# A fused attention and expert kernel: weight halves of batch 1 kept in DRAM for batches 2 and 3, and another order of reads and routing steps on VectorE

## What is computed

```python
def _L1_xattn_ref(x, context, Wq, Wkv, null_kv, Wout, ln_scale, ln_bias):
    q = _split_heads(jnp.einsum('bnd,df->bnf', x, Wq))
    kv = jnp.einsum('bmc,cf->bmf', context, Wkv)
    k, v = jnp.split(kv, 2, axis=-1)
    ...
    k = jnp.concatenate((nk, k), axis=-2)
    v = jnp.concatenate((nv, v), axis=-2)
    sim = jnp.einsum('bhid,bhjd->bhij', q * scale, k)
    attn = jax.nn.softmax(sim, axis=-1)
    out = jnp.einsum('bhij,bhjd->bhid', attn, v)
    out = jnp.einsum('bnf,fd->bnd', out.transpose(0, 2, 1, 3).reshape(b, -1, INNER), Wout)
    ...
x = x + jnp.tanh(g_xattn[1]) * _L1_xattn_ref(_layernorm(x, axis=-1), ctx_2048, ...)
x = x + jnp.tanh(g_ffn[1]) * _L1_ffn_ref(_layernorm(x, axis=-1), ...)
```

## Time and profile before

| | us |
|---|---|
| median of 3 runs | 1813.59 (1813.05 to 1813.76) |
| the profiled execution, its own time | 1819.89 |
| its span, first to last instruction | 1818.2 |

### The profile page before, as it was taken

How to read it: one execution, slowest core, us unless ns; L and a number is a source line. 1 busy time by engine, 2 the same in 40 slices (tenths; PEclk the granted TensorE clock), 3 DMA queues, 4 the chain that set the end, 5 groups by cost and what they waited for, 6 DMA issues and landing times. The chain is left out here.

```text
span 1818.2 us, 28277 instructions
## 1 busy us (share of the span) xinstructions
PE 1675.6 (92%) x9558; PEld 1135.1 (62%) x9558; DVE 1244.6 (68%) x2892; ACT 1076.3 (59%) x2214; POOL 421.2 (23%) x422
## 2 busy tenths in 40 slices
PE   5899998899799899999998999999998889999998
PEld 3445554455455344446665666566665788999997
DVE  3867876877778667576768667776685688666632
ACT  2467666666666655666656556566565466667621
POOL 2101110120011011020102010401021467777721
PEclk8899999999999999999999999989999999999999
DMA  3000000000002009320102010201012647777775
GB/s 104 1 24 1 1 24 1 1 24 7 1 1 104 36 1 311 112 67 18 42 18 65 19 39 30 89 18 41 13 43 87 215 135 225 207 216 193 220 228 163
DMA packets 143567, 142.88 MB, mean 79 GB/s; under 512 B 10816, under 2 KB 135744, under 8 KB 143424
## 3 DMA queue, kind: packets, MB, share of 16 engines
q1 hardware_dynamic: 135696, 132.41, 23.2%
q0 software_dynamic: 7152, 8.66, 2.7%
q10 hardware_dynamic: 576, 0.00, 0.0%
HBM read 112.18 MB, written 29.77 MB: 78 GB/s over the span
## 5 line engine op out<-in xcount | busy, mean ns | idle before, releaser
L1273 DVE TENSOR_REDUCE l_tile_max<-psum 128x1 f32<-128x512 f32 x512 | 342.0, 688 | 110.5 <-PE psum L951 108.8
L1121 ACT ACTIVATE l_probs<-psum 128x1024 f32<-128x1024 f32 x256 | 248.3, 1022 | 106.1 <-PE psum L963 102.3
L951 PE MATMUL psum<-l_kT,l_qT 128*128 128x512 f32 x512 | 238.1, 472 | 40.2 <-DVE l_tile_max L1273 36.8
L2047 ACT ACTIVATE l_probsT<-psum 128x1024 f32<-128x1024 f32 x128 | 131.1, 1024 | 140.2 <-PE psum L1926 135.1
L2973 POOL TENSOR_TENSOR moe_w_lo<-moe_w,moe_w_hi 128x512 fp32r<-128x512 f32 x128 | 179.4, 1403 | 95.2 <-ACT moe_w_hi L2757 94.1
L951 PEld LDWEIGHTS psum<-l_kT,l_qT 128*128 128x128 f32 x512 | 98.1, 193 | 132.1 <-DVE l_tile_max L1273 111.6
L2191 DVE TENSOR_REDUCE l_row_max<-psum 128x2 f32<-128x1024 f32 x124 | 151.0, 1218 | 35.5 <-PE psum L1763 35.0
L1983 ACT ACTIVATE l_probs<-psum,l_neg_max 128x512 f32<-128x512 f32 x248 | 168.3, 679 | 0.0
L963 PE MATMUL psum<-l_qT,l_kT 128*128 128x512 f32 x512 | 160.5, 397 | 1.7 <-ACT l_probs L1121 1.5
L2788 ACT ACTIVATE moe_gate<-psum 128x256 f32<-128x256 f32 (+1 forms) x184 | 64.6, 351 | 158.6 <-PE psum L2686 97.7
L2686 PE MATMUL psum<-moe_xs_hi,moe_w_hi 128*128 128x256 f32 x512 | 148.1, 289 | 1.6 <-DVE moe_xs_lo L2814 1.6
(11 more groups left out here) (394 smaller groups left out, 3496.8 us busy)
## 6 DMA issues: line engine op xcount, KB each, us to landing
moe_w<-in_moe_w SPq DMA_DIRECT2D x276, 256.0 KB, 4.7
moe_sorted_x<-l_null_cols SPq DMA_DIRECT2D x1, 17680.0 KB, 56.2
moe_w<-in_wkv SPq DMA_DIRECT2D x6, 1024.0 KB, 5.2
moe_w<-in_wkv SPq DMA_DIRECT2D x24, 256.0 KB, 2.7
moe_xs<-moe_sorted_x SPq DMA_DIRECT2D x16, 272.0 KB
moe_w<-in_ctx SPq DMA_DIRECT2D x8, 512.0 KB, 3.6
moe_w<-in_wkv SPq DMA_DIRECT2D x2, 2048.0 KB, 15.6
moe_w<-in_wq SPq DMA_DIRECT2D x24, 128.0 KB, 2.3
```

Of the source, the lines that this page charges most:

```text
L951: nc.tensor.matmul(bank(max_bank(m)), qT[:, q % SLOTS, h, t * P:(t + 1) * P], kT[:, q % SLOTS, h // 2, half * BANK:(half + 1) * BANK], sta ...
L1121: nc.scalar.activation(probs[:, n % PT_RING], wide(2 * (n % 2)), ACT.Exp, scale=SCALE).then_inc(exp_done, 1)
L1273: nc.vector.reduce_max(tile_max[:, q % 2, t, h, half:half + 1], bank(max_bank(m)), AX_X).then_inc(max_read, 1)
L2047: nc.scalar.activation(probsT[:, m % 2], wide(4).rearrange("p (j n) -> p j n", j=2), ACT.Copy).then_inc(pT_ready, 1)
```

## The change

- In batch 1, after a group's halves are made, SyncE writes them to three new DRAM tensors (`keep_queries`, `keep_keys`, `keep_values`), and waits for these writes before the buffers are loaded anew.
- In batches 2 and 3 SyncE loads hi and lo directly (two DMAs in place of one, twice the bytes), and TensorE waits for the loads. ScalarE's rounding and VectorE's subtractions for queries and keys end with group 15, GpSimd's for the values with batch 1.
- In batch 1 the subtraction for the values moves from GpSimd to VectorE: four instructions of 128x512 at (5, 2), (5, 3), (6, 1), (6, 2) of batch 0 and four at (2, 0) to (2, 3) of batch 1. GpSimd keeps the copies.
- VectorE reads the fill (i, 2, 1) before `extra` rather than behind it.
- In batches 1 and 2 `token_statistics` for the router moves from (5, 2), (5, 3), (6, 0) to (6, 1), (6, 2), (6, 3), and `route_tokens` from (6, 1), (6, 2) to (7, 0), (7, 1).

```diff
                 def load_queries(i):
+                    slot, p = i % 2, i % PAIRS
+                    if i >= 2 * PAIRS:
+                        sp.dma_start(wq_hi[:, slot].bitcast(F32), kept_wq[p, 0]).then_inc(wq_in[slot], 16)
+                        sp.dma_start(wq_lo[:, slot].bitcast(F32), kept_wq[p, 1]).then_inc(wq_in[slot], 16)
+                    else:
+                        cols = slice(p * P, (p + 1) * P)
+                        sp.dma_start(wq_raw[:, slot], dram["wq"][:, cols].rearrange("(c p) n -> p c n", p=P)).then_inc(wq_in[slot], 16)
...
+                def keep_queries(i):
+                    sp.wait_ge(wq_split, i - PAIRS + 1)
+                    sp.dma_start(kept_wq[i % PAIRS, 0], wq_hi[:, i % 2].bitcast(F32)).then_inc(wq_kept, 16)
+                    sp.dma_start(kept_wq[i % PAIRS, 1], wq_lo[:, i % 2].bitcast(F32)).then_inc(wq_kept, 16)
...
                 for n in range(PAIRS - 1, GROUPS):
                     b, p = divmod(n - 2, PAIRS)
+                    new = PAIRS <= n < 2 * PAIRS
                     coming = (n + 1, n + 2) if n == PAIRS - 1 else (n + 2,) if n + 2 < GROUPS else ()
+                    if new:
+                        keep_queries(n)
                     sp.wait_ge(misc_psum, last_fill("q", n))
+                    if new:
+                        sp.wait_ge(wq_kept, 32 * (n - PAIRS + 1))
                     for i in coming:
                         load_queries(i)
+                    if new:
+                        keep_keys(n)
...
                 def project_queries(i):
                     p = i % PAIRS
-                    if i >= PAIRS:
+                    if i >= 2 * PAIRS:
+                        pe.wait_ge(wq_in[i % 2], 16 * (PAIRS // 2) + 32 * ((i - 2 * PAIRS) // 2 + 1))
+                    elif i >= PAIRS:
                         pe.wait_ge(wq_split, i - PAIRS + 1)
...
                 def round_soon(i):
                     b, p = divmod(i, PAIRS)
-                    if PAIRS <= i + 2 < GROUPS:
+                    if PAIRS <= i + 2 < 2 * PAIRS:
                         round_keys(i + 2)
...
-                def split_values(b, half):
+                def round_values(b, half):
                     pool.wait_ge(wv_in, 16 * (2 * (b - 1) + half + 1))
                     for c in range(s.CC):
-                        nc.gpsimd.tensor_copy(wv_hi[:, c, :], wv_raw[:, c, :])
-                    pool.drain()
-                    for c in range(s.CC):
-                        nc.gpsimd.tensor_tensor(wv_lo[:, c, :], wv_raw[:, c, :], wv_hi[:, c, :].bitcast(F32),
-                                                ALU.subtract).then_inc(wv_split, 1)
+                        nc.gpsimd.tensor_copy(wv_hi[:, c, :], wv_raw[:, c, :]).then_inc(wv_rounded, 1)
...
+                def split_values(i, r):
+                    b, p = divmod(i, PAIRS)
+                    first = {(5, 2): 0, (5, 3): 1, (6, 1): 2, (6, 2): 3}
+                    if (p, r) in first and b == 0:
+                        b, half, c = 1, 0, first[p, r]
+                    elif p == 2 and b == 1:
+                        half, c = 1, r
+                    else:
+                        return
+                    dve.wait_ge(wv_rounded, s.CC * (2 * (b - 1) + half) + c + 1)
+                    nc.vector.tensor_tensor(wv_lo[:, c, :], wv_raw[:, c, :], wv_hi[:, c, :].bitcast(F32),
+                                            ALU.subtract).then_inc(wv_split, 1)
...
-                        route_at = 16 if soon else 22
+                        route_at = 16 if soon else 25
...
                         if i + 1 < GROUPS and r >= 1:
                             normalize(i + 1, r - 1)
+                        if r == 2:
+                            read_fill((i, 2, 1))
                         extra(*divmod(i, PAIRS), r)
+                        split_values(i, r)
                         if i + 1 < GROUPS and r == 3:
                             normalize(i + 1, r)
-                        if r >= 2 and not tokens_now:
+                        if r == 3 and not tokens_now:
                             read_fill((i, r, 0))
-                        read_fill((i, r, 1))
-                        if r == 2 and PAIRS <= i + 3 < GROUPS:
+                        if r != 2:
+                            read_fill((i, r, 1))
+                        if r == 2 and PAIRS <= i + 3 < 2 * PAIRS:
                             split_queries(i + 3)
```

More of the change, by code:

```diff
@@ L1647, in layer1 @@
         wq_in = [sem(f"l1_wq_in_{i}") for i in range(2)]
+        wq_kept = sem("l1_wq_kept")
+        wk_kept = sem("l1_wk_kept")
+        wv_kept = sem("l1_wv_kept")
         wq_rounded = sem("l1_wq_rounded")
@@ L1653, in layer1 @@
         wv_in = sem("l1_wv_in")
+        wv_rounded = sem("l1_wv_rounded")
         wv_split = sem("l1_wv_split")
@@ new lines, in load_values @@
+                def load_values(b, half):
+                    if b >= 2:
+                        sp.dma_start(wv_hi[:].bitcast(F32), kept_wv[half, 0]).then_inc(wv_in, 16)
+                        sp.dma_start(wv_lo[:].bitcast(F32), kept_wv[half, 1]).then_inc(wv_in, 16)
+                    else:
+                        cols = slice(s.I1 + half * BANK, s.I1 + (half + 1) * BANK)
+                        sp.dma_start(wv_raw, dram["wkv"][:, cols].rearrange("(c p) n -> p c n", p=P)).then_inc(wv_in, 16)
@@ L1704, in load_context, with keep_values @@
+                def keep_values(half):
+                    sp.wait_ge(wv_split, s.CC * (half + 1))
+                    sp.dma_start(kept_wv[half, 0], wv_hi[:].bitcast(F32)).then_inc(wv_kept, 16)
+                    sp.dma_start(kept_wv[half, 1], wv_lo[:].bitcast(F32)).then_inc(wv_kept, 16)
                 def load_context(b):
@@ L1791, in project_keys @@
                         pe.wait_ge(ctx_ready, 16)
-                    if b >= 1 and chunks[0] == 0:
+                    if b >= 2 and chunks[0] == 0:
+                        pe.wait_ge(wk_in[i % 2], 16 * (PAIRS // 2) + 32 * ((i - 2 * PAIRS) // 2 + 1))
+                    elif b >= 1 and chunks[0] == 0:
                         pe.wait_ge(wk_split, i - PAIRS + 1)
@@ L1805, in values @@
                 def values(b, half, kt):
-                    if b >= 1 and kt == 0:
-                        pe.wait_ge(wv_split, s.CC * (2 * (b - 1) + half + 1))
+                    if b >= 2 and kt == 0:
+                        pe.wait_ge(wv_in, 32 + 32 * (2 * (b - 2) + half + 1))
+                    elif b >= 1 and kt == 0:
+                        pe.wait_ge(wv_split, s.CC * (half + 1))
                     some = slice(kt * P, (kt + 1) * P)
```

48 lines of the change are left out of this document (33 added, 15 removed).

## The result

| | kernel before | changed kernel |
|---|---|---|
| median of six runs | 1813.18 (1808.9 to 1813.76) | 1797.59 (1789.34 to 1798.68) |
| ratio, 95% interval | | 0.9904 (0.988 to 0.9927) |
| repeated in a later group of runs (`e11_after`) | 1819.96 (1815.53 to 1825.3) | 1800.69 (1797.28 to 1804.57) |
| ratio there | | 0.9889 (0.9867 to 0.9911) |
| the profiled execution, its own time | 1819.89 | 1797.64 |

The change is worth 15.6 us by the first medians and 19.3 by the second.

The account below looks back on a forecast made before the run. PE, busy 689 of layer1's 720 us, bounds the kernel; only its idle time and lost clock can return. Waits 12 + clock 8.5 - costs 1.4 - 0.4 = 18.7 us, rounded to 18.5: median 1795.1 us, range 1786 to 1808.

Parts of the forecast that it names:

- waits for k_lo: Key-fill reads at 804, 981 and 1075: waits behind GpSimd's subtraction go, 0.8 + 1.6 + 1.9 = 4.3 us.
- waits for xT half 0: At (5, 2): 1.85 of 2.66 and 1.5 of 2.29 us go, plus 0.8 at 807 and 986; 4.15 us.
- null waits: At (6, 2): VectorE reads the fill 1.4 us earlier, so the 1.03 us wait goes in two batches, 2.1 us.
- waits for q_lo: Before the first half of the keys: 0.74 us waits in two batches, matched by a 0.68 us subtraction; 1.4 us.
- costs (new waits for probabilities): VectorE's added work: 1.4 us for two of eight subtractions, 0.4 for the nine small steps at (6, 3).
- clock: Falls at 984, 1072 and 1180 go (6.8 us), 1.7 more at the two null fills; 8.5 us, between 0 and 10.2.
- GpSimd's subtraction: Removed, VectorE is no longer 2.6 us late at (p, 1); three of six places give 4.3 us.
- The fill read before the extra work: Taken with moved router statistics at (5, 2), 807 and 986: 4.15 us of waits go.
- The nine small steps: About 2.1 us leaving (6, 0) for (6, 3); the 1.03 us waits at (6, 2) go; cost put at 0.4.
- Loads, stores, SyncE: Doubled loads for groups 16 to 31, and the stores, come early enough beside TensorE's work: all at 0.
- The 6.3 us between the profile and the median: Median of before lies 6.3 us below its profiled execution; the same difference turns the forecast 1801.4 into 1795.1.
- rival 3: ACT's two waits (1.85, 1.97 us) beside POOL's scatters go too: 24 us gained, 1789.6; chance 0.09.

Follow-up runs that it names:

- e11_after: The changed kernel, unchanged, run and profiled again in a later group of runs: 1800.69 us, ratio 0.9889 to the kernel before.
- e5_before: The kernel before, nothing edited, profiled a second time: span 1814.7 us in place of 1818.2.
- e2_values: Kernel before with only the values' halves kept and their subtraction moved to VectorE: 1809.14 us, ratio 0.9968.
- e6_early: Kernel before with only the fill (i, 2, 1) read ahead of the extra work: 1811.07 beside 1813.36 us, ratio 0.9992.
- e12_route: Kernel before with only the router's statistics and routed tokens planned three places later: 1810.41 beside 1819.96 us, ratio 0.9948.
- e3_qk: Kernel before with only the halves of queries and keys kept, values and order as before: 1813.33 us, ratio 0.9989.
- e4_kept: Changed kernel with both order edits (early fill read, later statistics) undone, all halves kept: 1806.16 us, ratio 0.9954 to the kernel before.
- e8_spread: Changed kernel with batch 0's value subtraction at (5, 3) moved to (6, 1): 1790.16 us, ratio 0.9871 to the kernel before.
- e9_traffic: Changed kernel with four 1 MB DRAM-to-DRAM copies ahead of each of four value loads: 1834.3 us, ratio 1.0093 to the kernel before.

## Why the prediction was right, point by point

The forecast was 1795.1 us; the medians were 1797.59, and 1800.69 where before takes 1819.96. The forecast difference of 18.5 us lies between the measured 15.6 and 19.3; for the profiled execution it was 1801.4, and 1797.64 was measured. PE's idle time and lost clock from 788 to 1348 are compared below for `e5_before` and the changed kernel, which both lack ACT's stops (waits over 0.45 us).

| step | forecast | `e5_before` to after |
|---|---|---|
| waits for k_lo | 4.3 | 0.96 + 1.63 + 1.74 + 0.82 = 5.2 |
| waits for xT half 0 | 4.15 | (0.81 - 0.54) + (2.66 - 0.88) + (2.72 - 0.53) = 4.2 |
| null waits | 2.1 | 2 x 1.04 = 2.1 |
| waits for q_lo | 1.4 | 2 x 0.74 = 1.5 |
| costs (new waits for probabilities) | 1.8 | (1.31 - 0.71) + 0.71 - (1.12 - 0.72) = 0.9 |
| clock | 8.5 | 13.6 - 5.1 = 8.5 |
| sum | 18.7 | 20.6; the layer itself: 20.0 |

The 13.6 us are falls of 1.7 at 824 and 984 and of 3.4 at 1004, 1072 and 1196. The two numbers of the last row don't cover the same stretch. The sum holds 0.6 us of batch 0, ahead of the first output projection; the layer's distance holds its end as well, where the changed kernel waits 0.8 us less for the probabilities (4.47 in place of 5.27) and loses 1.7 us more to the clock. That makes 19.1 of the 20.0; the remaining 0.9 us is not traced further.

**GpSimd's subtraction: right, with help at 1075.** `e2_values` removes these waits, but puts 1.53 us of waiting for the router's logits in the place of the one at 1075. The 1.9 us that the prediction booked there for the subtraction alone come only together with the order edits. A fourth wait, 0.82 us at 1173, isn't in the first profile of before, which has ACT's stop at 1164 just ahead of it; that the stop gave VectorE the time is likely, and not shown.

**The fill read before the extra work: right sum, wrong cause.** The 4.15 us were given to the read being early. `e6_early` shows that this alone hands 2.15 us on to the probabilities and gains nothing that can be told, and `e12_route` that the later statistics do it alone. The working looked at what stands ahead of the read and not at where it goes; the last reader behind it was the one to follow.

**The nine small steps: right as far as tested**, the null waits go when the statistics move (`e12_route`) and stay where they don't move (`e2_values`, `e3_qk`, `e4_kept`, `e6_early`); the key subtraction of 0.68 us, named beside them, has no part in it (`e3_qk`). No run moves the nine steps without the rest of the statistics. Their cost at (6, 3) was put at 0.4 us; no wait over 0.45 us stands there after.

**The clock: right in size, in part by luck.** The falls at 984 and 1072 went, 5.1 us as forecast. The 1.7 us forecast for 1180 are not in the measured 8.5: `e5_before` has no fall there, with a wait of 2.72 us ahead of the place (PEclk 1.00 from 1174 to 1190). In their stead the falls at 1004 and 1196 to 1208 both shrank from 3.4 to 1.7 us, where the forecast had taken 1.7 us for the two together. Against the first profile of before the clock gives 12.0 us, 10.3 without the 1.7 beside ACT's stop. Since a fall can be there or not in two executions of one kernel, the single terms of the clock are not confirmed by this. The three that are left each stand beside a null fill with no wait at it, as the one at 824 in the earlier trace rows. The Trainium skill (TensorE: Matmul & The Clock Gate, Part 1) lets the clock go by how busy the array has lately been. Taken strictly, as the prediction did, that would have kept the falls that hold narrow fills and made it 1800.2 us; the one at 1072, with the 128x8 matmuls, went all the same (PEclk 1.00 at 1068 to 1080).

**Costs on VectorE: within the bounds.** One subtraction of eight cost something, 0.6 us at 812, not two; `e8_spread` takes it away. The sign that the prediction named for moved work on the path, a wait for the probabilities of over 0.5 us, did come at three places (1.31, 0.71, 0.72), but only these 0.6 us are the moved work: `e12_route`, without any subtraction moved, has 0.71 at the second place as well.

**Loads, stores, SyncE: right.** No projection waits for a DMA, with 21 MB more moved: the page has 163.9 MB in place of 142.9.

**The 6.3 us between the profile and the median: carried over as a constant, which was wrong in kind.** Some 4.6 us of that one execution stood beside ACT's stops, and single executions of before spread from 1807.29 to 1825.3 us anyway. The changed kernel's profile was 0.05 us from its median. So the forecast of the profile was 3.8 us too high and that of the median 2.5 too low, and that the median came this close is in part luck. The pair of profiles, with the stops on one side only, shows 22.3 us, and reads as if rival 3 had come true. It had not: `e5_before` and `e11_after` show the stops gone and back without any edit.

**The experts' part** was held at its length. It is 4.0 us longer in the first pair (1818.2 - 1419.5 = 398.7 and 1795.9 - 1393.2 = 402.7). That this is an effect of the change isn't shown: `e5_before` has 401.8 and `e6_early` 398.2, from runs of the same code there.

## What to carry to other kernels

Before a read is moved ahead of other work on the same engine, follow that work to the reader behind it: here moving the read alone handed the wait on (`e6_early`), and moving the work to a later step removed it (`e12_route`). Take a second profile of the kernel before, and compare over a stretch between two fixed instructions, before a wait that ends with a "remote" is put down to the change. Where transfers are issued from one queue in order, look for the transfer with the least lead behind a new one: here it was the context that came late, and not the weights (`e9_traffic`).

## What the runs showed of the hardware

- ACT's stops of 2.0 to 6.6 us beside GpSimd's indirect scatters are in five of the profiles, around the last of eight scatters, and missing in the other nine with the same scatters. 32 MB more traffic away from the scatters brings no further stop (7.5 us in two stops, both times). Their cause stays open. The Trainium skill (SBUF — State Buffer, Who interferes with whom) says that DMA never contends with a compute engine; that no stop stands beside the copies of `e9_traffic` agrees with it.
- The granted clock falls to 1.2 GHz for 1.7 us' worth in windows in which PE is never idle (0.86 over 12 us at 820 and 996 after), and the same place with the same work keeps 2.4 GHz in another execution (1.00 from 1178 to 1190 in `e11_after`).
- VectorE's subtraction of 128x512 takes 0.68 us where GpSimd's takes 1.3 (four in 5.3) and holds VectorE up by 2.6 us meanwhile; moving it to the busier engine, together with keeping the halves of the values, gained 5.6 us (`e2_values`). The Trainium skill (SBUF — State Buffer, SBUF: two separate sides) says of the ports that VectorE and GpSimd share, which a VectorE instruction with two inputs in SBUF needs beside a GpSimd instruction that reads SBUF, that whoever comes first keeps them for the whole instruction; the trace agrees, as VectorE's small instruction with two inputs takes 1.16 us in place of 0.16 beside GpSimd's of 1.3 each.
